# Selective scan on one core: the skip term u·D goes into the matmul sum of y, and ScalarE copies the finished sum

## What is computed

```
xz = x @ W_in;  x_in, z = split(xz)
u  = silu(causal_conv(x_in, conv_w) + conv_b)          # 512 channels
dt = softplus(u @ W_dt + b_dt)
Bm, Cm = split(u @ W_x)                                 # 16 states each
h_t = exp(dt_t * A) * h_(t-1) + (dt_t * u_t) * B_t      # per channel and state
y_t = sum over the 16 states of h_t * C_t
y = y + u * D                                           # the skip term
out = layernorm(x + (y * silu(z)) @ W_out)
```

## Time and profile before

| | |
|---|---|
| time, median of 3 runs | 4757.71 us (4749.96 to 4757.81) |
| profiled execution, its own time | 4754.88 us |
| its span, first to last instruction | 4753.1 us |
| mean granted TensorE clock in it | 0.94 of full speed |
| DVE busy | 3515.1 us (74%) |
| PE busy | 3702.3 us (78%) |
| scan stage of the first block | 2129.5 to 2573.8 us |

### The profile page before, as it was taken

How to read it: one execution, slowest core, us unless ns; L and a number is a source line. 1 busy time by engine, 2 the same in 40 slices (tenths; PEclk the granted TensorE clock), 3 DMA queues, 4 the chain that set the end, 5 groups by cost and what they waited for, 6 DMA issues and landing times. The chain is left out here.

```text
span 4753.1 us, 41481 instructions
## 1 busy us (share of the span) xinstructions
PE 3702.3 (78%) x14192; PEld 2169.9 (46%) x14192; DVE 3515.1 (74%) x5187; ACT 1325.3 (28%) x2104; POOL 1536.6 (32%) x746
## 2 busy tenths in 40 slices
PE   5899879887988798777777677777777776777769
PEld 2697559755966496622223322223322233222234
DVE  4486448544864486469998679996699986799965
ACT  3102210221022202243332343331533323433310
POOL 1101200120103010306664036661066640366620
PEclk9999889988998899889999899998999998899989
DMA  3000200020002000204442124442044421244421
GB/s 119 1 1 1 72 1 1 1 72 1 1 1 72 1 1 1 94 17 153 155 154 89 54 90 155 154 153 69 14 151 155 154 94 54 83 152 155 152 66 36
DMA packets 140513, 350.03 MB, mean 74 GB/s; under 512 B 19698, under 2 KB 56946, under 8 KB 140034
## 3 DMA queue, kind: packets, MB, share of 16 engines
q1 hardware_dynamic: 140290, 347.19, 21.6%
HBM read 320.90 MB, written 26.26 MB: 73 GB/s over the span
## 5 line engine op out<-in xcount | busy, mean ns | idle before, releaser
L1314 POOL TENSOR_TENSOR hc<-h,c_sb 128x1024 f32<-128x1024 f32 x512 | 1205.8, 2355 | 1093.9 <-DVE h L1336 1067.2
L1265 PE MATMUL PS<-hc,ident 128*128 128x512 f32 x2048 | 1031.7, 627 | 490.0 <-POOL hc L1314 477.5
L1265 PEld LDWEIGHTS PS<-hc,ident 128*128 128x128 f32 x2048 | 354.0, 192 | 996.7 <-POOL hc L1314 743.9
L1291 ACT ACTIVATE da<-dt,a_neg 128x1024 f32<-128x1024 f32 x512 | 584.0, 1141 | 572.3 <-DVE h L1336 572.3
L1322 DVE TENSOR_TENSOR PS<-dtu,PS 128x1024 f32<-128x1024 f32 x512 | 618.6, 1209 | 7.8 <-PE PS L1248 7.8
L1336 DVE TENSOR_TENSOR_SCAN h<-da,state,PS 128x1024 f32<-128x1024 f32 x256 | 598.9, 2341 | 0.0
L1336 DVE TENSOR_TENSOR_SCAN h<-da,PS 128x1024 f32<-128x1024 f32 x256 | 583.0, 2277 | 0.0
L100 POOL TENSOR_TENSOR ln_rstd<-ln_var,eps_pow 128x4 f32<-128x4 f32 x65 | 71.5, 1105 | 924.8 <-DVE ln_var L93 924.8
L1248 PE MATMUL PS<-bc,pick 128*128 128x512 bf16 x1024 | 315.1, 392 | 47.9 <-PEq L1029 30.9
L687 DVE SCALAR_TENSOR_TENSOR acc<-PS,rw,acc 128x192 f32<-128x192 f32 x768 | 275.2, 412 | 51.3 <-PE PS L658 40.2
L658 PE MATMUL PS<-wmoh_hi,xhi 128*128 128x384 f32 x1024 | 272.9, 348 | 45.7 <-POOL xlo L635 45.7
(11 more groups left out here) (240 smaller groups left out, 5689.8 us busy)
## 6 DMA issues: line engine op xcount, KB each, us to landing
c_sb<-c_rows SPq DMA_DIRECT2D x512, 512.0 KB, 3.6
xT<-in_xT SPq DMA_DIRECT2D x16, 512.0 KB, 6.7
tok<-in_x SPq DMA_DIRECT2D x4, 2048.0 KB, 13.5
x_after_layer<-tok SPq DMA_DIRECT2D x16, 512.0 KB, 3.0
xT_after_layer<-xT SPq DMA_DIRECT2D x16, 512.0 KB, 3.9
x2T<-xT_after_layer SPq DMA_DIRECT2D x16, 512.0 KB, 7.0
tok<-x_after_layer SPq DMA_DIRECT2D x4, 2048.0 KB, 14.0
out<-tok SPq DMA_DIRECT2D x16, 512.0 KB, 2.9
```

Of the source, the lines that this page charges most:

```text
L1265: op = pe.matmul(bank(Y + j), ident[:, :], hc[:, v % 2, j * CHUNK:(j + 1) * CHUNK], start=(n == 0), stop=(n == N - 1))
L1291: act.activation(da[:, v % 2, :], dt[:, m, at], ACT.Exp, scale=a_neg[:, n:n + 1]).then_inc(dr, 1)
L1314: pool.tensor_tensor(hc[:, v % 2, :], h[:, v % 2, :], c_sb[:, v % 3, :], ALU.mult).then_inc(hr, 1)
```

## The change

The skip term is no longer added by DVE. In the setup of layer 1 DVE makes `skip`, four 128 x 128 diagonal matrices with the values of D. In each round PE opens the sum in Y with `through_skip(r)`: two float32 matmuls skip·u with start=True. They carry the wait on yd that the first gather had, and all 16 gathers now add. `collect_y` moves from DVE to ACT, where it is a plain copy from PSUM, written behind decay(v+2) of the unit n = 1; the last one of a block stands at the end of ACT's list.

```diff
+            skip = tile(W, "skip", [P, KI, P])
...
+                    for m in range(KI):
+                        dve.tensor_scalar(skip[:, m, :], ident[:, :], dskip[:, m:m + 1], None, ALU.mult)
...
                 def gather(v):
                     r, n = units[v]
                     pe.wait_ge(hr, v + 1)
-                    if n == 0 and r:
+                    for j in range(2):
+                        op = pe.matmul(bank(Y + j), ident[:, :], hc[:, v % 2, j * CHUNK:(j + 1) * CHUNK],
+                                       start=False, stop=(n == N - 1))
+                    op.then_inc(yr, 1)
+
+                def through_skip(r):
+                    m, _, at = where(r)
+                    if r:
                         pe.wait_ge(yd, r)
                     for j in range(2):
-                        op = pe.matmul(bank(Y + j), ident[:, :], hc[:, v % 2, j * CHUNK:(j + 1) * CHUNK],
-                                       start=(n == 0), stop=(n == N - 1))
-                    op.then_inc(yr, 1)
+                        pe.matmul(bank(Y + j), skip[:, m, :], u[:, m, at.start + j * CHUNK:at.start + (j + 1) * CHUNK],
+                                  start=True, stop=False)
...
                     if v + 3 <= last:
                         spread_b(v + 3)
+                    r, n = units[v]
+                    if n == 0:
+                        through_skip(r)
                     gather(v)
...
+                def collect_y(r):
+                    m, _, at = where(r)
+                    act.wait_ge(yr, N * (r + 1))
+                    act.activation(dt[:, m, at], bank(Y, 2), ACT.Copy).then_inc(yd, 1)
+
                 decay(0)
                 decay(1)
-                for v in range(len(units)):
+                for v, (r, n) in enumerate(units):
                     save(v)
                     if v + 2 <= last:
                         decay(v + 2)
+                    if n == 1 and r:
+                        collect_y(r - 1)
+                collect_y(len(rounds) - 1)
...
-                def collect_y(r):
-                    m, _, at = where(r)
-                    dve.wait_ge(yr, N * (r + 1))
-                    dve.scalar_tensor_tensor(dt[:, m, at], u[:, m, at], dskip[:, m:m + 1], bank(Y, 2), ALU.mult,
-                                             ALU.add).then_inc(yd, 1)
...
                     if v < last:
                         times_u(v + 1)
-                    if n == 1 and r:
-                        collect_y(r - 1)
                     scan(v)
-                collect_y(len(rounds) - 1)
```

More of the change, by code:

```diff
@@ L994, in layer1 @@
                 with ExitStack() as s:
-                    state_space(nc, b, s, tile, sem, bank, ident, tok, w_in, w_dt, w_x, w_out, cw, cb, bdt, dskip,
+                    state_space(nc, b, s, tile, sem, bank, ident, tok, w_in, w_dt, w_x, w_out, cw, cb, bdt, skip,
                                 a_neg, pick, bc3, x2_dram, x2T_dram, c_dram, kept, layer_norm, out)
@@ L999, in layer1, with state_space @@
             experts(nc, t, out, s, tile, sem, bank, ident, ones, kept, layer_norm)
-def state_space(nc, b, s, tile, sem, bank, ident, tok, w_in, w_dt, w_x, w_out, cw, cb, bdt, dskip, a_neg, pick, bc3,
+def state_space(nc, b, s, tile, sem, bank, ident, tok, w_in, w_dt, w_x, w_out, cw, cb, bdt, skip, a_neg, pick, bc3,
                 x2_dram, x2T_dram, c_dram, kept, layer_norm, out):
```

## The result

The changed kernel takes 4856.02 us (median of 4 runs, 4853.05 to 4857.82), the kernel before 4754.7 us (4 runs).

The account below looks back on a forecast made before the run. DVE was taken to bound the scan stage. 4754.9 us + 55 (stall) + 59 (clock) + 3 (block starts) - 1 (block ends) = 4871, forecast as a median of 4873 us; 8-in-10 range 4805 to 4905.

Parts of the forecast that it names:

- The path: Between rounds: copy waits behind decay, PE idles, then skip matmuls, gather and spread delay times_u(4); one stall a boundary.
- The stall without the clock: At the 28 round boundaries: times_u(4) 2.03 us later in half 0, 1.9 in half 1, together +55 us.
- The clock: PE's idle time lowers its clock on the chain behind, at nearly all 28 boundaries: 2.1 us each, +59 us.
- my two prices: Loss per clock fall: 1.7 us for 3.4 us at half speed, 2.9 us for 5.9 us.
- the last copy of a block gives back 1: At the 4 block ends ACT's copy replaces DVE's 1.28 us collection: 4 x 0.26 = 1 us gained.
- The rival of a steady clock: The stall comes, the clock does not fall or only sometimes: 4815 us, up to about 4830; chance 0.13.
- The start of a block: First skip matmuls of a block stand in front of gather(0) at low clock: 0.75 us a block, +3 us.
- The deciding rival: ACT takes the copy before the decay that waits for scan(1), so it comes early enough: 4719 us, faster; chance 0.05.

Follow-up runs that it names:

- The early copy: Changed kernel with ACT's copy of y moved ahead of the save of n=1 and the decay of n=3: 4713.33 us, ratio to before 0.992.
- the run with PE kept busy: Changed kernel plus useless bf16 spread matmuls while PE would wait for the late copy: 4802.14 us, ratio to before 1.011.
- the copy alone: Changed kernel with the late copy on ACT but the skip term left out of the computation: 4802.66 us, ratio to before 1.010.
- both with the skip matmuls in the middle: Changed kernel with skip matmuls behind the gathers of n=8 and n=9: copy late 4806.05 us; copy ahead of save and decay 4714.71 us.
- the kernel with the copy behind the save: Changed kernel with ACT's copy behind the save of n=1 but ahead of the decay of n=3: 4743.55 us, ratio to before 0.998.

## Why the prediction was right, and where it was off

**The path was right at each step.** Copy behind the decay, PE idle for about 4 us, skip matmuls, gather and spread in a row, one stall at times_u(4), none behind it. The early copy shows the cause: it removes all of it. The step on which all hung, that ACT would not take the copy past the waiting save and decay, is in the trace: the last gather was over at 2188.78 (2186.80 + 1.98), ACT stood idle from 2188.84 to 2190.90, and the copy began at 2192.05. (The unit of 3.31 us is 1.12 + 2.19; "twice 1.12" in the forecast is a slip of words and not of the sum.)

**The stall without the clock: forecast +55 us, found +48.** From the first product with dt·u to the last one, a scan stage takes 433.5 us before and 445.5 in the run with PE kept busy; four of them make 48 us. The forecast had a stall of 3.45 us for half 0, and 3.1 was found. Some 0.2 us of the difference lie in the handovers: the copy starts 0.09 us before the decay ends (2191.01 + 1.13 against 2192.05), and PE follows ACT within 0.05 us, where I had taken the 0.14 us that it needed behind DVE.

**The clock: forecast +59 us, found +52.** The same stretch takes 458.5 us in the changed kernel, 13.0 more than with PE kept busy; the two runs' times differ by 54. Of my two prices the one for a short fall, 1.7 us, was found, and the one for a long fall was 2.9 for 3.05. I took 2.1 as the mean; the long fall came only once in 7 boundaries, and 52 / 28 is 1.9 us. That the mean came out so near is in part luck: how often a fall would be long stood in no row. The rival of a steady clock is ruled out: after idle times of 3.9 us it fell at all 28, where before it fell behind 6 of the 28.

"TensorE: Matmul & The Clock Gate" in the Trainium skill, section "HAM oscillation — how this bites in real kernels", says that a PE idling between bursts starts each burst throttled. The trace agrees in that each burst pays, with 28 falls in 28. It differs in the start: at 20 of them the burst began at 1.00 and the clock fell 0.5 to 1.2 us later, at the other 8 it had fallen 0.1 to 0.7 us before.

**The start of a block: forecast +3 us, found about -1.** The wait there fell from 0.61 us to 0.36, and the clock came back 3.4 us sooner. I put this down to the skip matmuls, which make PE busier there: in the three runs without them at that place (the copy alone and both with the skip matmuls in the middle) the wait is 0.61 again. The four diagonal matrices kept DVE busy for 4.5 us, not for 0.9 (one of them took 3.9), and yet cost nothing: the first scan stage starts at 2129.6, and at 2129.9 before.

**The sum.** The 48 and 52 make 100 us, with the starts of the blocks in them. Up to the first product of the next stage it is 98.9 of the 102.5 (473.66 against 448.93 us in each block): the last copy of a block gives back 1, as forecast. The other 3.6 lie in the stages outside. Over all ten profiles that time outside lies anywhere between 3011 and 3022 us, so 3.6 need no cause in the change.

**The deciding rival** had its point right. A copy that ends about a microsecond after the last gather keeps nearly all of the gain: forecast 4719 us, measured 4713.

## What to carry to other kernels

Moving work from the engine that bounds to an idle one pays only if the receiver can start it in time. Look at what stands ahead of it in that engine's list and what that waits for, not at how idle the engine is. When a resource has one buffer, put its release ahead of everything that waits for something later; the skip matmuls behind an early release were free, and behind the late one they were paid in full (50 us for 28 x 1.82). And look at PE's idle time ahead of a chain that others wait for twice: once as time, and once for the low clock that may follow. It followed at all 28 boundaries after 3.9 us of idle time, and at 4 of the 12 after 2.86 us in the kernel with the copy behind the save.

## What the runs showed of the hardware

- Useless matmuls sped the kernel up: 8 added pairs of bf16 matmuls at each of 28 boundaries held the granted clock at 1.00 and took 54 us off.
- The low clock falls mostly on the work behind an idle time and not on the idle time. At the first boundary it was still 1.00 while PE idled (2189.21 to 2193.10) and 0.50 only from 0.6 us after the skip matmuls began. At the last one of a block it was 0.50 for the last 0.7 us of the idle time and for 6.1 us of work.
- PE followed ACT's copy by 0.05 us and DVE's copy by 0.05 us too (2187.93 + 1.23 to 2189.21), but the old collection by 0.14. There the matmul waited for two semaphores, POOL's product and the collection. Two waits alone do not make the difference: the first gather in the run with the copy alone waits for both as well and follows the copy by 0.05 us (2190.35 + 1.00 to 2191.41). There the product had been ready for 3 us, in the kernel before for 0.05 us; whether that is the reason stays open.
